# One VectorE reduction over j in place of three VectorE adds and one GpSimd add, with all call orders changed

## What is computed

```
q, k, v = x @ Wq, x @ Wk, x @ Wv;  fg = sigmoid(x @ Wf + bf)      # (b, s, 16 heads, 8)
for each t:  state[i, j] = state[i, j] * fg[i] + v[i] * k[j]
             out[i]      = sum over j of state[i, j] * q[j]
out = layernorm(out) * gamma + beta;  out = (out * silu(x @ Wg)) @ Wout
x   = layernorm(x + out)
h   = silu(x w1) * (x w2);  h = gelu(h h1);  h = gelu(h h2);  y = h w3     # 128 -> 512 -> 512 -> 512 -> 128
x   = layernorm(x + y)
```

## Time and profile before

| | |
|---|---|
| median of 3 runs | 522.09 us (521.32 to 525.92) |
| span of the profiled execution | 520.7 us |
| PE busy | 502.3 us, 96% |
| DVE busy | 453.9 us, 87% |
| ACT busy | 403.9 us, 78% |
| POOL busy | 317.8 us, 61% |
| DMA | 87.33 MB, mean 168 GB/s |

### The profile page before, as it was taken

The page is one execution under the profiler, slowest core; times in us unless marked ns, Lnnn a source line. Parts: engine busy times, 40 slices in busy tenths (PEclk is TensorE's granted clock), DMA queues, the critical chain, the costliest instruction groups (busy, mean ns, idle before and its releaser), DMA issues. The chain is left out here.

```text
span 520.7 us, 7950 instructions
## 1 busy us (share of the span) xinstructions
PE 502.3 (96%) x2524; PEld 382.6 (73%) x2524; DVE 453.9 (87%) x707; ACT 403.9 (78%) x837; POOL 317.8 (61%) x363
## 2 busy tenths in 40 slices
PE   8999999999999999999999999999999998999995
PEld 5466777787876767787877777687767777767885
DVE  4699899999999998999999989999998999991462
ACT  3567778789797688889888787889788878678754
POOL 0642755839394765938295775858496775838351
PEclk9999999999999999999999999999999999999999
DMA  6987998972998748895597963699947747400001
GB/s 197 257 230 165 250 230 217 230 166 77 211 232 218 174 133 199 211 237 162 128 233 196 265 167 70 166 228 234 237 108 196 180 131 177 107 1 2 21 22 43
DMA packets 21500, 87.33 MB, mean 168 GB/s; under 512 B 2512, under 2 KB 3280, under 8 KB 13520
## 3 DMA queue, kind: packets, MB, share of 16 engines
q1 hardware_dynamic: 21312, 86.53, 66.7%
q10 hardware_dynamic: 144, 0.26, 0.1%
HBM read 74.72 MB, written 12.06 MB: 167 GB/s over the span
## 5 line engine op out<-in xcount | busy, mean ns | idle before, releaser
L474 POOL TENSOR_TENSOR h1lo<-h,h1hi 128x512 fp32r<-128x512 f32 x60 | 77.7, 1313 | 27.4 <-ACT h1hi L891 27.1
L898 ACT ACTIVATE h<-F,cols 128x512 f32<-128x512 f32 x120 | 79.0, 686 | 9.4 <-PE F L2303 8.9
L542 POOL TENSOR_TENSOR QJ<-QJ 128x512 f32<-128x512 f32 x14 | 18.0, 1285 | 102.6 <-DVE QJ L1589 102.6
L474 POOL TENSOR_TENSOR h2lo<-h,h2hi 128x512 fp32r<-128x512 f32 x60 | 76.1, 1298 | 5.6 <-ACT h2hi L891 5.5
L1574 DVE TENSOR_TENSOR_SCAN KJ<-g,KJ 128x512 f32<-128x512 f32 x64 | 74.8, 1203 | 3.7 <-POOL KJ L523 3.2
L1574 DVE TENSOR_TENSOR_SCAN KJ<-g,carry,KJ 128x512 f32<-128x512 f32 x64 | 77.8, 1261 | 0.3 <-ACT carry L824 0.2
L2303 PE MATMUL F<-h2hi,whi 128*128 128x512 f32 (+1 forms) x256 | 73.4, 421 | 1.8 <-DVE h2hi L1694 1.0
L1581 DVE TENSOR_TENSOR QJ<-QJ,KJ 128x1024 f32<-128x1024 f32 x60 | 75.0, 1275 | 0.0
L2303 PE MATMUL F<-h1hi,whi 128*128 128x512 f32 (+1 forms) x256 | 69.8, 413 | 3.8 <-DVE h L1638 3.8
L2303 PE MATMUL F<-h1lo,whi 128*128 128x512 f32 (+1 forms) x256 | 67.1, 404 | 0.0
L2303 PE MATMUL F<-h2lo,whi 128*128 128x512 f32 (+1 forms) x256 | 66.0, 400 | 0.0
(11 more groups left out here) (176 smaller groups left out, 947.7 us busy)
## 6 DMA issues: line engine op xcount, KB each, us to landing
KJ<-qk_bounce SPq DMA_DIRECT2D x30, 1024.0 KB, 11.2
QJ<-qk_bounce SPq DMA_DIRECT2D x30, 1024.0 KB, 11.4
qk_bounce<-qk SPq DMA_DIRECT2D x30, 256.0 KB, 3.1
x_in<-in_x SPq DMA_DIRECT2D x16, 256.0 KB, 7.8
xT<-in_xT SPq DMA_DIRECT2D x15, 256.0 KB, 4.6
out<-res SPq DMA_DIRECT2D x15, 256.0 KB, 3.1
wraw<-in_wffn SPq DMA_DIRECT2D x2, 1024.0 KB, 10.5
wraw<-in_wffn SPq DMA_DIRECT2D x2, 256.0 KB, 4.3
```

The source lines that it names most:

```text
L474: e.tensor_tensor(h_lo[layer][:, t, :w], h[:, t, :w], h_hi[layer][:, t, :w].bitcast(f32), ALU.subtract).then_inc(lo_done[layer], 1)
L542: e.tensor_tensor(first, first, other, ALU.add).then_inc(add_gp_done, 1)
L898: e.activation(dst[:, t, :WIDTH[n]], F[t][:, :WIDTH[n]], ACT.Gelu, scale=scale[t]).then_inc(gelu_done[layer], 1)
```

## The change

`add`, `add_gp` and their semaphores go. `sum_rows(n)` comes, for blocks 2 to 15: one `tensor_reduce` on VectorE over all eight rows. Its input is `QJ` read as (partition, token, j), with j innermost: eight elements that lie 2,048 bytes apart are read and summed, then the next token's eight. It reads 4096 elements a partition and writes 512 into `o_norm`, which `norm_o` overwrites later in the same block; so it also waits until TensorE has transposed the `o_norm` of the block ahead (`yT_made`). `sum_transposed` then reads `o_norm` in place of row 0 of `QJ`.

```diff
-            def add_gp(n):
-
-                e.wait_ge(add_done, adds(n + 1))
-                first, other = (rows(QJ, n)[:, k, :] for k in (0, 1))
-                e.tensor_tensor(first, first, other, ALU.add).then_inc(add_gp_done, 1)
...
-            def add(n, p):
-
-                e.wait_ge(qs_done, NPAIR * (n - 1) + p + 2)
-                if p:
-                    e.wait_ge(add_done, adds(n) + p)
-                first, other = (rows(QJ, n)[:, 2 * k:2 * k + 2, :] for k in (0, p + 1))
-                e.tensor_tensor(first, first, other, ALU.add).then_inc(add_done, 1)
+            def sum_rows(n):
+
+                e.wait_ge(qs_done, NPAIR * n)
+                e.wait_ge(yT_made, n)
+                e.tensor_reduce(o_norm[:, :WIDTH[n]], rows(QJ, n).rearrange("p j t -> p t j"), mybir.AxisListType.X,
+                                ALU.add).then_inc(sum_done, 1)
...
-                    e.wait_ge(add_gp_done, adds_gpsimd(n + 1))
+                    e.wait_ge(sum_done, summed(n + 1))
...
-                        last = e.matmul(back[:, chunk(c)], rows(QJ, n)[:, j, chunk(c)], ident[:], is_transpose=True,
+                        src = rows(QJ, n)[:, j, chunk(c)] if n in EARLY else o_norm[:, chunk(c)]
+                        last = e.matmul(back[:, chunk(c)], src, ident[:], is_transpose=True,
                                         start=j == 0, stop=j == terms - 1)
...
             load_projections(0)
+            load_weights(0)
+            load_xT(1)
+            load_constants()
```

More of the change, by code:

```diff
@@ L121, in kv_gpsimd, with summed @@
             return sum(4 if m in EARLY else 2 for m in range(1, n))
-        def adds_gpsimd(n):
+        def summed(n):
             return sum(m not in EARLY for m in range(1, n))
-        def adds(n):
-            return sum(0 if m in EARLY else ADDS for m in range(1, n))
         def landed(n):
@@ L1911, in _ @@
             scan(7, 6)
+            kv(8, 0)
             scan(7, 7)
+            qs(7, 0)
             qs(7, 1)
+            x1_lo(6)
             qs(7, 2)
-            x1_lo(6)
             qs(7, 3)
-            add(7, 0)
-            add(7, 1)
+            sum_rows(7)
             hmul(6, 0)
-            add(7, 2)
             hmul(6, 1)
             residual_2(5)
-            kv(8, 0)
+            scan(8, 0)
             hmul(6, 2)
@@ L1926, in _ @@
             stats_o(7)
-            scan(8, 0)
             kv(8, 1)
@@ L1970, in _ @@
             qs(9, 3)
-            add(9, 0)
-            add(9, 1)
+            sum_rows(9)
             hmul(8, 0)
-            add(9, 2)
             hmul(8, 1)
-            kv(10, 0)
             residual_2(7)
@@ L1995, in _ @@
             qs(10, 2)
+            qs(10, 3)
             x1_lo(9)
-            add(10, 0)
-            qs(10, 3)
-            add(10, 1)
-            add(10, 2)
+            sum_rows(10)
             hmul(9, 0)
@@ L2049, in _ @@
             qs(12, 2)
-            add(12, 0)
+            qs(12, 3)
             x1_lo(11)
-            qs(12, 3)
-            add(12, 1)
-            add(12, 2)
+            sum_rows(12)
             hmul(11, 0)
+            kv(13, 0)
+            residual_2(10)
             hmul(11, 1)
-            residual_2(10)
-            kv(13, 0)
+            stats_o(12)
             hmul(11, 2)
-            stats_o(12)
             hmul(11, 3)
@@ L2076, in _ @@
             qs(13, 2)
+            qs(13, 3)
             x1_lo(12)
-            add(13, 0)
-            qs(13, 3)
-            add(13, 1)
+            sum_rows(13)
             hmul(12, 0)
-            add(13, 2)
             hmul(12, 1)
@@ L2086, in _ @@
             hmul(12, 2)
+            stats_o(13)
             hmul(12, 3)
-            stats_o(13)
             scan(14, 0)
             kv(14, 1)
+            scan(14, 1)
             kv(14, 2)
-            scan(14, 1)
             scan(14, 2)
+            qs(14, 0)
+            residual_1(13)
+            stats_1(13)
             scan(14, 3)
@@ L2096, in _ @@
             scan(14, 5)
-            residual_1(13)
-            stats_1(13)
             scan(14, 6)
             scan(14, 7)
-            qs(14, 0)
             qs(14, 1)
+            x1_lo(13)
             qs(14, 2)
-            x1_lo(13)
-            add(14, 0)
             qs(14, 3)
-            add(14, 1)
-            add(14, 2)
+            sum_rows(14)
+            residual_2(12)
             hmul(13, 0)
             hmul(13, 1)
-            residual_2(12)
             stats_o(14)
```

1228 lines of the change are left out of this document (606 added, 622 removed).

## The result

| | before | after |
|---|---|---|
| median time, us | 522.55 | 577.48 |
| lowest to highest, us | 521.32 to 525.92 | 576.86 to 580.0 |
| profiled span, us | 520.7 | 575.2 |

Both are medians of four runs. The ratio is 1.1057, with a 95% interval from 1.1013 to 1.1102: the change makes the kernel 10.6% slower. The forecast was 529 us, and the time lies above the upper end of the range, 560.

The account below looks back on a forecast made before the run. The prediction took a loop of 29.36 us a block with DVE full to 95% as the bound; 522.1 + 5.9 (thirteen blocks at +0.45) + 1.0 (last block) gave 529 us, range 518 to 560.

Parts of the forecast that it names:

- What bounds the kernel: Blocks 0 to 12: a 29.36 us loop, DVE busy 27.99, idle 1.37, the rest handed back and forth with PE and ACT.
- What goes: 3.60 us a block: DVE in each block: three adds of 1217 ns go, which hold the engine for 3.60 us.
- The reduction: 4.34 us taken: DVE's new sum of 4096 elements, bounded from 4.34 to 8.47 us; lower bound taken, +0.74 us a block.
- The 553 us that the prediction estimated from the page's number: Kernel time if DVE's reduction took 7.2 us, by the skill page's 1.73 ns a column for a hopping source.
- Where it lies: Block 8, around `hmul(7, 0)`: 0.74 us later, 0.7 of PE's 1.5 us slack left, no new PE stall; sum 2.4 sooner.
- What comes back: 0.29 of 0.58: DVE's waits for transposed sum, last product and `attention_out`, 0.58 us a block: half given back, so a block costs +0.45.
- The last block: +1.0: `x1_lo(14)` to `hmul(14, 3)`: +1.66, less up to 1.14 from an earlier start; +1.0 us taken, between 0.5 and 1.7.
- Moves: 0: Reordered loads at the start, the new `yT_made` wait and GpSimd meeting `qs`: 0 taken, 2 us of range.
- The fear that GpSimd would meet `qs`: GpSimd, no longer parked, may lengthen DVE's `qs`: up to +1 us a block; 0 kept, 2 us of range.
- Rival B: DVE's reduction reads slowly: 573 us at the upper bound, 544 halfway; chance 0.25, of which 0.08 above 560.
- What would show it: Signs: reduction row 4.4 us for A, C or D, 6 or more for B; mark spacing above 30.5 for B; GpSimd's add wait gone.

Follow-up runs that it names:

- The probes: The kernel before with nine VectorE operations (reductions, a multiplication, an addition, in various read patterns) at its end; 560.45 us, one run, only its rows used.
- the run with eight neighbours: The changed kernel with the reduction reading eight neighbours instead of eight elements 2,048 bytes apart, summing wrong elements; 526.79 us, ratio 1.0065.

## Why the prediction was wrong, point by point

- **What bounds the kernel.** The loop of 29.36 us with DVE full to 95% and the rest passed back and forth with PE was right, and so was that PE's 96% do not show its room. What the forecast did not see is that both are near the limit at once: with the orders of after, the curve has its knee at about the forecast's own 4.3 us of summing, and 1 us less would have gained almost nothing.
- **What goes: 3.60 us a block.** Right, as far as the runs show: at full rate DVE is busy 28.40 us a block, 0.41 more than before, where the sum gives +0.74 and `qs` takes 1221 ns in the mean (1275 before, about four a block), which accounts for 0.2 of the missing 0.3.
- **The reduction: 4.34 us taken, 7.34 measured. This is the step that failed.** It was bounded from 4.34 to 8.47, and I went with the lower bound because of ScalarE's `save_carry` on eight elements and of the single addition a step. The addition was rightly no cause: a maximum is as slow, and neighbours are added at full rate. The witness was too weak to speak. The probes put 0.7 ns an element between fast and slow on DVE; for eight elements that is 5.6 ns, and the two rows that I compared are 6 ns apart, so they could as well be read as slow. It was also another engine. The Trainium skill ("Vector Engine (DVE) Microarchitecture Reference", section 5.2) stood against it with a number of 7.2 us, measured now as 7.16 and 7.42; of its two sentences I leaned towards the one on two regions, and the pattern has eight. The 553 us that the prediction estimated from the page's number is too low for its own sum, too: with 7.2 us, 7.12 of the engine, that estimate is 522.1 + 13 x (3.52 - 0.29) + 3.8 = 568, and about 554 comes out only if all of DVE's idle time goes first.
- **Where it lies.** Of PE's 1.5 us of slack in front of tile 2, 0.7 were to be left. For block 8 this looked at the wrong place, a second step that failed: there the new order has the transposed sum ahead of tile 2, and it waits for `residual_2`, behind the reduction and `hmul(7, 0)`. At full rate that is just in time: `residual_2` is over at 265.30 and the transposes start at 265.45 behind PE's own last product, so no stall was right there, with next to nothing left and not 0.7. With 3 us more PE stood still 2.99 us at block 8 and 9.6 us in all in front of the transposes for `residual_2`, in three blocks, beside 29.4 us (5.8 before) for `hmul`, in most of the others.
- **What comes back: 0.29 of 0.58.** At full rate the block came out at 29.84 with 29.81 forecast, so the size holds as a sum. But that is luck, for it was made up differently from what I wrote: DVE's busy part is 0.3 less than 28.7, and its idle part is 1.44 and not 1.08, so the waits gave nothing back.
- **The last block: +1.0.** Between `x1_lo(14)` and `hmul(14, 3)` the forecast had +1.66, and took off what `x1_lo(14)` itself could come sooner. With the slow reduction the 1.66 becomes 4.66, and 5.8 was measured; the forecast had no idle time left there, and DVE waits 0.24, 0.61 and 0.27 us between the two (timeline of that stretch), 1.12 together, which closes it.
- **Moves: 0.** In the sum with everything else it held at full rate; by themselves the moves were not measured there. And it is no constant: with the slow reduction the orders are worth 35 us, and with adds in place of it they lose time against the kernel before (540.78, 535.21, 543.06), for which DVE's longer adds give only part. The fear that GpSimd would meet `qs` did not come true here, `qs` is even shorter (1223 ns in the mean, 1275 before); GpSimd meets adds that stand where the reduction stands.
- **Rival B** named the mechanism and had a chance of 0.25, but its prices in time were too low. It had 573 for 8.47 us of reduction. For 7.34 its formula, all of the idle time going first, gives 522.1 + 13 x (3.74 - 1.37) + 4.7 = 558, and 577.48 was measured. The forecast's own way, nothing more given back than 0.29, gives 522.1 + 13 x (3.74 - 0.29) + 4.0 = 571. The 19 us between 558 and 577 lie in the twelve blocks: with all idle time gone one would take 27.99 + 3.74 = 31.73 us, and it took 33.29. The idle time did not go but grew, from 1.37 to 1.87 us, while DVE's busy part stayed 0.31 below that sum. Since B was priced so low, the range of 518 to 560, meant to leave out only its far end, left out the true time.
- **What would show it.** The row of the reduction (over 6 us) and the spacing of the marks (33.3, over 30.5) said B at once. GpSimd's wait for adds is gone, as forecast.

How much of PE's loss is its waiting and how much its halved clock can be told in part. Between the run with eight neighbours and the changed kernel the twelve blocks grow by 41.5 us: 28.1 are gaps of PE (7.2 to 35.3), and 13.4 are longer busy time for the same matmuls, with 3.4 and 27.3 us at half clock in the stretch. Gaps also come nearly without it: the new order with four adds has 14.9 us of them with the same 3.4 us at half clock. What stays open is how many of the gaps come back to PE from its own slower products by way of DVE's waits. None of the kernels tried is faster than the one before.

## What to carry to other kernels

One operation in place of four is no saving if it reads the same elements in an order that the engine reads slowly; price an access pattern by a row that has the pattern on the same engine and is long enough to show the difference, and where there is none, give the slow price its full weight. Where two engines hand work to each other and both are near full, more work on one does not use up all of its idle time first: here DVE's fell from 2.28 to 1.24 us a block, and then grew to 1.87 because PE stalled and in part came back at half its clock.

## What the runs showed of the hardware

- A DVE reduction over fp32 reads at full rate (1.04 ns an element) from neighbours, with 8 bytes between elements' starts, and from two regions in turn; with 16 bytes, or with four or eight regions in turn, it takes 1.69 to 1.75. In the working kernel it took 7425 ns, 4% more than the 7160 when the other engines had little to do.
- A multiplication by a constant reads groups of four that hop 2,048 bytes at 0.94 ns an element (not measured on neighbours; a copy takes 0.53), the addition of two such inputs at 1.80 (1.04 in order).
- DVE's adds with two inputs rise from 1217 to about 2180 ns when they start while GpSimd is at work on two inputs (eight of 42 in two kernels); the multiplications beside them rise from 1294 to as much as 2377, two of them not at all. The reductions, with GpSimd at work beside them in the changed kernel, never did (7376 to 7497). By "SBUF — State Buffer", section "Who interferes with whom", in the Trainium skill the first meets GpSimd's reads and the second does not; the runs agree with both.
- Around a stop of PE of 2.99 us the granted clock fell to 0.50 (1.2 GHz). Of the 14 stops of 2.36 to 4.08 us in the changed kernel nine went with such a fall, one of 2.36 us among them, and five of 2.44 to 2.79 us did not. In the span there were 35.5 us of this, 66.6 in the kernel with the reduction in the old order, 1.3 before.
